# The last pair's routing placed inside the first expert blocks, products without a reader in the last rounds, and a result load queued behind all row loads

## The reference

```
x = x + conv(groupnorm(x))        # a 7x7 depthwise filter per image, itself computed from the image
t = tokens(x)                     # 256 tokens of 128 features per image
t = t + attention(layernorm(t))   # q = tanh(z), softmax(q q^T / sqrt(128)) z, per image
t = t + experts(layernorm(t))     # 8 experts, each token uses the best 2
...
scores = xf @ router_w + router_b
probs  = softmax(scores);  topk_p, topk_i = top_k(probs, 2)
h      = xf @ w1[e] + b1[e]
gated  = silu(h @ wg[e] + bg[e]) * (h @ wv[e] + bv[e])
y      = gated @ w2[e] + b2[e]
out    = sum over the token's two experts of topk_p * y
```

## Time and profile before

| | |
|---|---|
| median of three runs | 336.23 us (335.49 to 338.3) |
| the profiled execution: time | 339.49 us |
| its span, first to last instruction | 337.4 us |
| its mean granted clock of TensorE | 0.95 |
| busy: PE, PEld, DVE, ACT, POOL | 293.9, 235.4, 233.6, 144.7, 164.4 us |
| chain that ended last, by engine | PE 70%, DVE 11%, DMA 6%, issue 4%, ACT 3%, SPq 3% |

### The profile page before, as it was taken

One profiled execution on the slowest core, in us unless ns is written; L12 is line 12 of the kernel. 1 busy time (PEld: TensorE's weight loads), 2 busy tenths in 40 slices (PEclk: granted clock), 3 DMA queues, 4 the chain that ended last, 5 costly groups with the idle time before them and its releaser, 6 DMA issues.

```text
span 337.4 us, 7076 instructions
## 1 busy us (share of the span) xinstructions
PE 293.9 (87%) x1701; PEld 235.4 (70%) x1701; DVE 233.6 (69%) x1012; ACT 144.7 (43%) x465; POOL 164.4 (49%) x187
## 2 busy tenths in 40 slices
PE   1889999999999999999977746999999999999720
PEld 1557777777877777787856644777888888887510
DVE  2434465588797888878886885787766766777563
ACT  1334334536253372524122223655666666665200
POOL 3001011021255646456755847577777777675440
PEclk9999999999999999999977975999999999999795
DMA  6753241230214500010111114334332434249518
GB/s 197 278 153 93 82 140 34 82 90 2 78 64 105 212 19 32 32 35 24 42 33 33 42 50 105 104 105 114 87 100 82 111 104 112 79 119 309 164 40 274
DMA packets 29920, 33.39 MB, mean 99 GB/s; under 512 B 5064, under 2 KB 23836, under 8 KB 29626
## 3 DMA queue, kind: packets, MB, share of 16 engines
q1 hardware_dynamic: 24608, 23.64, 24.4%
q0 software_dynamic: 4352, 8.60, 7.5%
q10 hardware_dynamic: 922, 0.71, 0.6%
HBM read 21.69 MB, written 11.68 MB: 99 GB/s over the span
## 4 chain that ended last, share of the span: by engine, by line
PE 70%; DVE 11%; DMA 6%; issue 4%; ACT 3%; SPq 3%; POOL 1%; DVEq 1%; ACTq 0%; POOLq 0%
PE bank L1162 9%; PE bank L1757 7%; PE bank L1079 6%; PE bank L1737 4%; PE bank L1172 4%; PE bank L1147 4%; PE bank L1732 4%; PE bank L1733 4%; PE bank L1154 4%; PE bank L1746 4%; PE bank L1116 2%; PE bank L1074 2%; PE bank L1727 2%; PE bank L1094 2%; DMA e_attn<-moe_dram 2%
## 5 line engine op out<-in xcount | busy, mean ns | idle before, releaser
L1466 POOL DMA_INDIRECT moe_dram<-ys,xs x71 | 69.7, 982 | 34.5 <-issue 18.2
L429 POOL DMA_INDIRECT rows_dram<-row,slot x56 | 55.7, 994 | 25.0 <-issue 13.5
L1757 PE MATMUL bank<-w_all,gatedt 128*128 x284 | 44.2, 279 | 0.1
L1554 ACT ACTIVATE silu<-bank 128x256 f32<-128x256 f32 x71 | 27.3, 384 | 36.1 <-PE bank L1737 35.3
L1689 DVE SCALAR_TENSOR_TENSOR gated<-bank,xs,silu 128x256 f32<-128x256 f32 x71 | 34.2, 482 | 10.1 <-ACT silu L1554 6.1
L1673 DVE SCALAR_TENSOR_TENSOR ys<-b_all,xs,bank 128x128 f32<-128x128 f32 x71 | 24.7, 348 | 23.8 <-issue 21.6
L1757 PEld LDWEIGHTS bank<-w_all,gatedt 128*128 128x128 f32 x284 | 37.9, 195 | 0.3 <-issue 0.3
L1732 PE MATMUL bank<-w_high,x_high 128*128 x71 | 35.2, 495 | 0.2 <-ACT x_high L1542 0.2
L1162 PE MATMUL bank<-zhat,const 121*128 121x256 f32 (+1 forms) x128 | 32.6, 412 | 1.1 <-DVE zhat L716 1.1
L1737 PE MATMUL bank<-w_high,x_low 128*128 x71 | 30.1, 424 | 0.4 <-DVE x_low L1664 0.2
L440 POOL TENSOR_TENSOR frstd<-fvar,minus_half 128x2 f32<-128x2 f32 x7 | 4.9, 706 | 51.5 <-DVE fvar L803 51.5
(11 more groups left out here) (203 smaller groups left out, 614.6 us busy)
## 6 DMA issues: line engine op xcount, KB each, us to landing
xs<-rows_dram SPq DMA_DIRECT2D x71, 66.0 KB, 2.0
xc<-in_x SPq DMA_DIRECT2D x8, 256.0 KB, 2.9
wgv<-in_wg SPq DMA_DIRECT2D x8, 256.0 KB, 2.7
wgv<-in_wv SPq DMA_DIRECT2D x8, 256.0 KB, 3.1
xt<-in_xt SPq DMA_DIRECT2D x4, 512.0 KB, 4.5
xt<-moe_dram SPq DMA_DIRECT2D x8, 256.0 KB, 3.5
moe_dram<-ys,xs POOLq DMA_INDIRECT x71, 2.4
const<-in_const SPq DMA_DIRECT2D x1, 1123.0 KB, 9.0
```

Of the source, the lines that this page charges most:

```text
L429: pool.indirect_dma_start(rows_dram, bass.IndirectOffsetOnAxis(ap=slot[:, f % 2, 2 * t + k:2 * t + k + 1], axis=0), row[:, f % 2, t, k, :] ...
L1466: pool.indirect_dma_start(moe_dram, bass.IndirectOffsetOnAxis(ap=xs[:, u, C + 1:C + 2].bitcast(U32), axis=0), ys[:, u, :], None, bounds_ch ...
L1554: act.activation(silu[:, j % 2, :], bank_h[j % 2][:, 0:HID], ACT.Silu).then_inc(S["silu_done"], 1)
L1757: last = pe.matmul(bank_y[j % 2][:, 0:C], gatedt[:, j % 2, h * P:(h + 1) * P], w2_all[:, bass.ds(e * (2 * C) + h * C, C)], start=(h == 0), ...
```

## The change

On PE nine calls of `keep_busy` with sixteen products in all come into the last rounds, and `ranks(7)` (`LAST` is 7) moves behind the products of block 1. On DVE the routing of pair 7 moves into the blocks: `first_choice(7)` behind block 0's low part, the rest in iterations 0 to 4, and each part of the second table one iteration later. On ACT block 0's `high_part` and then pair 7's exp go ahead of the first Silu, before which ACT loads another function table. On POOL the eight scatters of pair 7 begin three blocks later. On SP the result loads of pairs 0 to 5 stand behind all row loads, four stores instead of three go ahead of the last results, and the next three stores wait until those results have landed; DVE sums pairs 0 and 1 within the blocks (iterations 66 to 69) and pairs 2 to 6 behind them.

```
@@ scalar
-                weights_exp(7)
-                experts["scalar"](act)
+                experts["scalar"](act, lambda: weights_exp(7))
@@ vector
-                    if 4 <= j <= 12 and j % 2 == 0:
-                        experts["second_table"](dve, j // 2 - 2)
+                    if 6 <= j <= 14 and j % 2 == 0:
+                        experts["second_table"](dve, j // 2 - 3)
...
-                first_choice(7)
-                second_choice(7)
-                slots_from_ranks(7)
-                experts["pad_places"](dve)
-                experts["vector"](dve, second_list)
+                def last_pair(j):
+
+                    if j == 0:
+                        first_choice(LAST)
+                    if j == 1:
+                        chosen_of(LAST)
+                        either_of(LAST)
+                    if j == 2:
+                        exp_sum_of(LAST)
+                        exp_reciprocal_of(LAST)
+                    if j == 3:
+                        weights_of(LAST)
+                        positions_of(LAST)
+                    if j == 4:
+                        chosen_positions_of(LAST)
+                        slots_of(LAST)
+                    if j == 5:
+                        slot_indices_of(LAST)
+                        experts["pad_places"](dve)
+                    second_list(j)
+
+                experts["vector"](dve, last_pair)
@@ tensor
                 router_input(5)
+                keep_busy(bank_s0[:, 0:2 * P], 1)
                 pe.wait_ge(pos_done, 5)
                 router(5)
+                keep_busy(bank_s0[:, 0:2 * P], 2)
                 pe.wait_ge(t1_done, 7)
                 image(7)
                 ranks(5)
                 features_of_z(6)
+                keep_busy(bank_d1[:, 0:2 * P], 1)
...
                 scores(6, 0)
                 scores(6, 1)
+                keep_busy(bank_d1[:, 0:2 * P], 2)
                 attention(6)
                 features_of_z(7)
+                keep_busy(bank_d1[:, 0:2 * P], 1)
...
                 scores(7, 0)
                 scores(7, 1)
+                keep_busy(bank_d1[:, 0:2 * P], 2)
...
                 router_input(6)
+                keep_busy(bank_d1[:, 0:2 * P], 1)
                 pe.wait_ge(pos_done, 6)
                 router(6)
+                keep_busy(bank_d1[:, 0:2 * P], 5)
                 router_input(7)
                 ranks(6)
+                keep_busy(bank_d1[:, 0:2 * P], 1)
                 router(7)
-                ranks(7)

                 def second_list(j):
+                    if j == 1:
+                        ranks(LAST)
@@ expert_programs, gpsimd
-            m, rest = divmod(j - 2, 3)
+            m, rest = divmod(j - 5, 3)
@@ expert_programs, sync
             sp.dma_start(xs[:, u, :], rows_dram[bass.ds(row0, P), :]).then_inc(xs_loaded[u], 16)
-            p = j - (NB - SPLIT)
-            if p == 0:
-                all_sent(sp, EARLY)
-            if 0 <= p < SPLIT:
-                load_result(sp, p, 0)
-                load_result(sp, p, 1)
-        for p in range(SPLIT // 2):
+        all_sent(sp, EARLY)
+        for p in range(SPLIT):
+            load_result(sp, p, 0)
+            load_result(sp, p, 1)
+        for p in range(4):
             store(sp, p)
         all_sent(sp, NB)
         for p in range(SPLIT, PAIRS):
             load_result(sp, p, 0)
-        for p in range(SPLIT // 2, PAIRS - 1):
+        sp.wait_ge(y_loaded[PAIRS - 1], 16 * 2)
+        for p in range(4, PAIRS - 1):
             store(sp, p)
@@ expert_programs, scalar
+        high_part(0)
+        weights_exp()
         act.activation(warm[:, :], ident[:, 0:1], ACT.Silu)
-        high_part(0)
@@ expert_programs, vector
         low_part(0)
+        second_list(0)
         for j in range(NB):
...
-            second_list(j)
-            p, k = divmod(j - (NB - 7), 2)
-            if 0 <= p < SPLIT // 2:
+            second_list(j + 1)
+            p, k = divmod(j - (NB - 5), 2)
+            if 0 <= p < 2:
...
-        for p in range(SPLIT // 2, PAIRS - 1):
+        for p in range(2, PAIRS - 1):
             first_sum(p)
             second_sum(p)
```

More of the change, by code:

```diff
@@ L1536, in sync, with scalar @@
         sp.wait_ge(S["stored"], 16 * (PAIRS + 1))
-    def scalar(act):
+    def scalar(act, weights_exp):
         def high_part(j):
```

## The result

| | before | after |
|---|---|---|
| median of the runs | 336.98 us (335.49 to 338.3, 4 runs) | 332.59 us (332.3 to 333.24, 4 runs) |
| ratio of the runs | | 0.988, interval 0.984 to 0.992 |
| the profiled execution: time, span | 339.49, 337.4 us | 332.57, 330.6 us |
| mean granted clock in it | 0.95 | 0.97 |

A ratio leaves out runs that took over 1.5% longer than the fastest of their kernel; a median has them all. The change is faster by 1.2%, or 4.4 us between the medians. The prediction had 329.0 us with a range to 332.5, so it expected too much, and the measured time lies just outside its range. The two profiled executions, by contrast, differ by 6.9 us, close to the 7.4 us of the prediction's sum. The gap between these two differences is what the experiments had to explain.

What follows compares the result with a forecast made beforehand. TensorE bounds the kernel, with low-clock stretches, the last pair's routing standing alone, and late last rows. 1.9 + 1.3 + 1.0 - 0.7 - 1.0 + 4.6 + 0.3 = 7.4 us gained: 328.8, said as 329.0 us, range 326.0 to 332.5.

Steps and rivals of the forecast that it cites:

- first rival: Clock's part missing: the low clock's place may vary by run, (a) and (b) worth nothing; gain 4.2 us, 332.0; chance 0.15.
- (f): Last blocks: all 71 row loads ahead of the result loads, so the stall goes; gain 4.6 us, bounds 3.8 and 5.5.
- (g): Tail: stores wait for the last results, one more pair summed behind the blocks; gain 0.3 us, bounds -0.7 and +1.0.
- (a): Before the last routing: filling products keep the last image at the full clock; gain 1.9 us, bounds 0 and 2.2.
- (b): Filled gap of 2.61 us keeps the last router_input and router at full clock; gain 1.3 us, bounds 0 and 1.4.
- queue limit in (a): `ranks(5)` and the features of z wait for VectorE's `either`; of 3.1 us less on TensorE, at most 2.2 arrive.
- (c): Block 0's gated row 5.2 us after the last router's end (R), not 6.2, table load on path; gain 1.0 us.
- (d): Blocks 0 to 4: VectorE's remaining routing, 2.3 us, partly exceeds its free time; loss 0.7 us, bounds 0 and 2.3.
- (e): Block 0: TensorE stands still some 2 us and the clock falls again; loss 1.0 us, bounds 0 and 2.5.
- the rival of block 14: Block 14's row load, behind later pads, comes late; TensorE waits up to 1.5 us; 331.5 to 332; chance 0.08.
- The slower rival: Filling products run at the low clock, overhang their gaps and delay the last routing stretch; 342.6 us; chance 0.03.
- the one with no gain at the end: At the last blocks, result loads stay in the way in another form; 333.4 us; chance 0.06.

Runs made afterwards that it cites:

- columns one and three of the table: Two profiled executions of the unchanged kernel before: the one used for the prediction (339.49 us, span 337.4) and a later third one (335.79 us, span 333.9).
- the first execution: The kernel before, unchanged, in the profiled execution used for the prediction: 339.49 us, span 337.4 us.
- the third: The kernel before, unchanged, profiled once more after the other experiments: 335.79 us, span 333.9 us.
- the change's second: The changed kernel, unedited, profiled and timed again: median 333.34 us (6 runs), ratio 0.989 against the kernel before.
- the filled experiment: The change plus four products without a reader behind block 0's last hidden product: 331.39 us (6 runs), 1.95 us less than the change.

## Why the prediction was wrong, and where it was right

**The step that failed** is the last of the sum: "The profiled execution took 339.49 us ... so 332.1 in its terms; the three timed runs have a median of 336.23, 3.3 us lower, which gives 328.8." In the terms of the profiled execution the change gave 332.57, half a microsecond from 332.1. But the 3.3 us by which that execution was longer could not be taken off once more, because, as far as the executions at hand tell, they lay in the parts that the change shortens: of the 3.5 us of span between columns one and three of the table 2.85 are in the end and 0.94 between `image(6)` and R, less small differences elsewhere. The kernel after has no such stall, and its profiled execution (332.57) is as long as its median run (332.59). The prediction saw the sign, "the timed runs lie 1.2 to 4 us under the profiled one", put it under its first rival, and there only to the clock.

**The term that carried it is (f).** 4.6 us, 4.9 with (g), was measured rightly on the one execution (16.83 to 11.81 us is 5.0, and 0.3 for the tail). In the runs the end is worth 2.2 us alone [1.1, 3.4] and 2.1 in company, as the middle one of the profiled old ends says too. Its bounds of 3.8 and 5.5 were both taken from that execution, so the range did not reach the usual case. How long the last rows take to land under full DMA engines decides it, and that changes between executions. What decides the landing itself stays open.

**The range** was also added up wrongly. The good ends of (a) to (g) add up to 11.7 us and not 10 (324.5 us, not 326). The bad ones add up to a loss of 1.7, so halfway from 7.4 to there is a gain of 2.9 us, or 333.4, and not 332. By the prediction's own bounds the range would have held the 332.59; its bounds for (f) would still not have held the 2.2.

**(a) and (b), the clock.** 3.2 us were expected; `image(6)` to R is 3.4 us shorter against the first execution and 2.4 against the third. In the runs the filling alone gave 3.7 us [1.4, 5.9], and 2.9 between the new end alone (0.993) and the new end with filling (0.985). The queue limit in (a) was right too: `ranks(5)` waits 0.83 us for `either` behind the faster image, so 3.0 us less on TensorE arrive only in part. Taken out of the whole change, the filling is worth 2.0 to 2.3. In all six profiled executions without the filling the clock was low under the last image, which took 5.38 to 6.73 us; in seven of the eight with it the image took 3.70, and in one, the change's second, 4.54. The first rival, that this part is missing, is refuted. That its 332.0 us came close to the measured 332.59 is chance: the part that it left out was there, and 2.7 us of the end, which it kept, were not. The Trainium skill ("TensorE: Matmul & The Clock Gate", What's actually happening) calls the gate's window free-running, so that a ramp moves from run to run; the trace agrees in kind, since the same image took 6.73, 6.55 and 5.85 us in three executions of the kernel before.

**(c), (d), (e), the routing.** Gated of block 0 came at R + 4.6, not R + 5.2, so (c) gained 1.6 and not 1.0. Blocks 0 to 16 lost 2.5 us against the first execution, where (d) and (e) had 1.7. Together a loss of 0.9, predicted 0.7. The clock's fall behind block 0 happened as foreseen, at 1.6 us by the profile of the filled experiment (1.95 by its runs) instead of 1.0. (d) took VectorE's shortest distance between two gated rows to be 1.17 us; the same trace has 1.09 further on, which changes little. What was missed is a comparison. Without filling, R to block 16 takes 32.2 us with the moved routing and 32.0 to 32.4 in five executions with the old one. With the clock held up to R it takes 33.3 to 33.5 with the moved one (three executions), 31.7 and 32.8 with the old one. So in company of (b) the move loses more. By the runs it is 0.5 without filling and 1.4 to 1.5 with it, against the predicted 0.7.

**(g), and what was costed at nothing.** The tail is 0.3 us shorter, as expected. The sums in iterations 66 to 69 cost close to nothing: the last down products but one stand 1.4 to 1.6 us apart. The pads moved to 215.53 us and the row load behind them to 224.49, where the rival of block 14 had 222; but the blocks ahead were later as well, and no transpose waited for rows there. The slower rival and the one with no gain at the end did not come either.

Put together from the runs: 2.2 for the end, 2.9 for the filling, 1.1 to 1.5 lost by the routing, 3.6 to 4.0 us; the whole was measured as 4.4 and 3.5 us between medians. These are three steps of one chain (new end, then filling, then routing), so that they add up shows nothing by itself. What supports them is that the first two were measured another way as well: 2.1 for the end, and 3.7 alone or 2.0 to 2.3 in company for the filling. The moved routing alone was not run. Of the 7.4 us of the sum the end thus lacks 2.7, the routing 0.4 to 0.8 and the filling 0.3.

One microsecond of the difference between the profiles belongs to none of these: the start to `image(6)` took 164.0 us in one and 165.0 in the other, and the three executions of before alone differ by 1.3 there.

## What to carry to other kernels

A profile is one execution: before its terms are subtracted from a median, ask which of them make that execution longer than the others, and take these off once only. A wait that a transfer ends under full DMA engines needs bounds from more than one execution, or from none to whole. Products without a reader paid here in gaps ahead of work that had run at the low clock, and a step that opens a new gap, such as a table load moved onto the path, has to bring its own; even then it has to be compared with the old order filled in the same way.

## What was not expected of the hardware

The load of the same 66 KB took 5.29 and 5.59 us to land in two executions, and at most 3.5 in a third, each time behind full DMA engines (0.99, 1.02 and 0.94 of their time in 308 to 312 us); the first and the third were issued at the same place. With result loads among the last row loads six or more runs of a kernel spread over 3.4 to 7.3 us, with the rows ahead and the sums moved as well over 1.6 to 3.0. An `ACT_TABLE_LOAD` took 1.28 us in each of six profiles, and the next instruction of ScalarE began within 0.02 us of its end, so the drain of part (c) of the prediction did not show.
